# One-hot columns in quarters, dense products of the last tile ahead of its pairs, and two joins of picked rows at other places of a macro tile

## The reference

```
e = stack([tbl_0[ids[:, 0]], ..., tbl_25[ids[:, 25]]], axis=1)          # 2048 x 26 x 128
combined = concatenate([dense[:, None, :], e], axis=1)                  # 2048 x 27 x 128
inter = einsum('bfd,bgd->bfg', combined, combined)                      # 27 x 27 per sample
z = concatenate([dense, inter[:, iu, ju]], axis=1)                      # 351 pairs, f < g
h = concatenate([z, dense], axis=1)                                     # 607
h = maximum(h @ W_top1 + b_top1, 0.0)                                   # 512
h = maximum(h @ W_top2 + b_top2, 0.0)                                   # 256
y = h @ W_top3                                                          # 2048 x 1
```

## Time and profile before

| | |
|---|---|
| median of 3 runs | 451.1 us (450.58 to 453.02) |
| the profiled execution | 452.48 us, of which its span 450.7 us |
| PE busy | 413.7 us (92%) |
| DVE, ACT, POOL busy | 312.7, 255.1, 236.2 us (69%, 57%, 52%) |
| PE's granted clock, mean | 0.992 |

### The profile page before, as it was taken

How to read it: one execution, slowest core, us unless ns; L and a number is a source line. 1 busy time by engine, 2 the same in 40 slices (tenths; PEclk the granted TensorE clock), 3 DMA queues, 4 the chain that set the end, 5 groups by cost and what they waited for, 6 DMA issues and landing times.

```text
span 450.7 us, 9538 instructions
## 1 busy us (share of the span) xinstructions
PE 413.7 (92%) x3496; PEld 392.5 (87%) x3496; DVE 312.7 (69%) x970; ACT 255.1 (57%) x577; POOL 236.2 (52%) x247
## 2 busy tenths in 40 slices
PE   0867799989999999999999899999999999998997
PEld 1756699979998899989998799988999799988976
DVE  4898498786777857776777857777777876744351
ACT  3785667383455745375454844466452945459462
POOL 5677355555655566655566456555565556653000
PEclk9999699999999999999999999999999999999999
DMA  6999514232233172322522153221533243111000
GB/s 183 251 237 263 123 50 93 73 62 63 85 75 81 40 98 62 78 65 61 86 67 80 44 85 70 76 78 43 100 71 67 64 70 73 42 42 31 1 2 0
DMA packets 25407, 36.47 MB, mean 81 GB/s; under 512 B 6197, under 2 KB 19645, under 8 KB 25362
## 3 DMA queue, kind: packets, MB, share of 16 engines
q1 hardware_dynamic: 17682, 20.13, 21.7%
q0 software_dynamic: 7680, 15.74, 13.8%
HBM read 35.84 MB, written 0.01 MB: 80 GB/s over the span
## 4 chain that ended last, share of the span: by engine, by line
PE 75%; DVE 7%; issue 5%; DMA 4%; ACT 4%; SPq 3%; DVEq 0%; ACTq 0%
PE gram_ps L481 22%; PE x_ps L463 16%; PE x_ps L464 15%; PE tail_ps L521 5%; DVE hot L942 5%; PE tail_ps L522 5%; PE tail_ps L523 4%; PE x_ps L443 4%; DMA raws<-in_tbl_dram 4%; PE tail_ps L514 2%; SPq L349 2%; ACT x L695 2%; DVE pairs L926 1%; DVE gram L926 1%; ACT pairs L695 1%
## 5 line engine op out<-in xcount | busy, mean ns | idle before, releaser
L410 POOL DMA_INDIRECT rows<-in_tbl_dram,ids_sb x240 | 235.4, 981 | 178.7 <-PE x_ps L463 63.5
L942 DVE TENSOR_SCALAR hot<-ids_all,row_f 125x256 fp32r<-125x256 int32 x636 | 193.0, 373 | 51.8 <-PE x_ps L464 29.3
L463 PE MATMUL x_ps<-hot,table_hi 125*128 125x256 f32 x656 | 169.3, 294 | 23.4 <-DVE table_lo L929 10.2
L464 PE MATMUL x_ps<-hot,table_lo 125*128 125x256 f32 x656 | 164.0, 285 | 0.0
L463 PEld LDWEIGHTS x_ps<-hot,table_hi 125*128 125x128 f32 x656 | 126.2, 192 | 29.6 <-issue 20.0
L464 PEld LDWEIGHTS x_ps<-hot,table_lo 125*128 125x128 f32 x656 | 126.5, 193 | 0.0
L481 PE MATMUL gram_ps<-x 128*108 128x108 f32 x1024 | 108.3, 259 | 0.9 <-issue 0.9
L481 PEld LDWEIGHTS gram_ps<-x 128*108 128x108 f32 x1024 | 102.9, 175 | 2.0 <-ACT x L695 0.7
L695 ACT ACTIVATE picked<-x_ps 128x256 f32<-128x256 f32 x88 | 33.6, 382 | 97.7 <-PE x_ps L464 75.6
L695 ACT ACTIVATE gram<-gram_ps 44x208 f32<-44x208 f32 (+3 forms) x136 | 46.0, 338 | 29.1 <-PE gram_ps L481 24.3
L926 DVE COPY gram<-gram_ps 44x208 f32<-44x208 f32 (+1 forms) x120 | 44.3, 369 | 13.1 <-PE gram_ps L481 9.3
(11 more groups left out here) (82 smaller groups left out, 414.8 us busy)
## 6 DMA issues: line engine op xcount, KB each, us to landing
ids_all<-in_selected_ids_dram SPq DMA_DIRECT2D x83, 128.0 KB
raws<-in_tbl_dram SPq DMA_DIRECT2D x11, 448.0 KB
rows<-in_tbl_dram,ids_sb POOLq DMA_INDIRECT x240
rows<-in_r_dense_features_dram SPq DMA_DIRECT2D x16, 64.0 KB
stage<-in_W_pairs_dram SPq DMA_DIRECT2D x1, 702.0 KB
ids_start<-in_selected_ids_dram SPq DMA_DIRECT2D x5, 128.0 KB
raws<-in_tbl_dram SPq DMA_DIRECT2D x11, 52.0 KB
stage<-in_W_dense_dram SPq DMA_DIRECT2D x2, 256.0 KB
```

The lines of the kernel that those rows point to most:

```text
L410: pool.indirect_dma_start(out=rows[t][:, slot, :], out_offset=None, in_=tables[GATHERED[slot - 1]], in_offset=bass.IndirectOffsetOnAxis(ap ...
L463: first = pe.matmul(bank, table_hi[j][:, c, :], v, start=(c == 0), stop=False)
L464: last = pe.matmul(bank, table_lo[j][:, c, :], v, start=False, stop=(c == VC - 1))
L942: last = dve.tensor_scalar(hot_buffers[hot_place(number)][:, c, :], ids, row, None, ALU.is_equal)
```

## The change

- One-hot columns come in quarters of two chunks. `HOTS` is 4, at the start there are 10 places of half the size, so the memory is the same. PE waits at chunks 0, 2, 4 and 6 and tells after each of the first three quarters that it has been read. At the start ACT still makes the second half of every odd table, its last step now in two instructions of 512 columns instead of one of 1024.
- `picked` is split. Tables 0 to 5 have a second place for the rows of tile 1, used in turn by the macro tiles (`picked_a`), so pick 0 needn't follow `join(m, 1, 0)`. This join now stands behind pick 3.
- `join(m, 0, 1)` stands behind pick 0 of its macro tile instead of between the copies of rows (0,0) and (0,1); for macro tiles 0 and 7 it stays.
- In the last macro tile both joins of tile 1 are DVE's, ahead of its first pair columns; the dense products of layer 1 go to four banks of `gram_ps` and stand ahead of the pair transposes (n = 0, 1) and ahead of layer 3 of the macro tile before (n = 2, 3).

The diff, without the repeated renaming of halves to quarters:

```diff
-    HALF = VC // 2
-    HOTS = 2
+    HOTS = 4
+    QUARTER = VC // HOTS
-    START_HOTS = 5
-    ACT_HOTS = [2 * j + 1 for j in range(1, NS, 2)]
+    START_HOTS = 10
+    ACT_HOTS = [hot_number(0, j, h) for j in range(1, NS, 2) for h in range(HOTS // 2, HOTS)]
-    LAST_BANKS = [2, 3, 2, 3, 0, 2, 3, 1, 0, 2, 3, 1, 0, 2]
+    LAST_BANKS = [2, 3, 2, 3, 0, 2, 3, 4, 5, 6, 7, 1, 0, 2]
-        picked = sb("picked", [D, NS, MACRO])
+        picked_a = sb("picked_a", [D, 1 + 2, IDS, P])
+        picked_b = sb("picked_b", [D, NS - IDS, MACRO])
+        tail_banks += [b[:, i, :] for b in gram_ps for i in range(UNIT_BANKS)]
+        def picked_rows(m, t, part):
+            if part == 1:
+                return picked_b[:, :, t * P:(t + 1) * P]
+            return picked_a[:, 0 if t == 0 else 1 + m % 2, :, :]
-                    if c == HALF - 1:
+                    if c % QUARTER == QUARTER - 1 and c < VC - 1:
                         last.then_inc(hot_read, 1)
...
+            def layer1_dense(m, n):
+                if is_last(m):
+                    pe.wait_ge(gram_moved[n // UNIT_BANKS], (m + 1) * UNITS)
                 bank = tail_bank(m, Q_H1 + n)[:, 0:MACRO]
                 cols = slice(n * P, (n + 1) * P)
                 pe.wait_ge(dense_kept, m + 1)
                 add_product(bank, ...)
...
                 layer2(m - 1, 0)
+                layer1_dense(m, 0)
+                layer1_dense(m, 1)
                 pair_transposes(m, 0)
                 pair_transposes(m, 1)
                 layer2(m - 1, 1)
                 pair_transposes(m, 2)
                 pair_transposes(m, 3)
+                layer1_dense(m, 2)
+                layer1_dense(m, 3)
                 layer3(m - 1)
...
             def macro_tile(m, before):          # ACT
                 transposes(m, 0, 2)
-                join(m, 1, 0)
                 pick(m, 0)
+                if m > 0:
+                    join(m, 0, 1)
...
                 pick(m, 3)
+                join(m, 1, 0)
                 if not before:
                     split_w2()
...
                 transposes(m + 1, 0, 0)
-                join(m + 1, 0, 1)
+                if is_last(m + 1):
+                    join(m + 1, 0, 1)
                 transposes(m + 1, 0, 1)
...
             def last_tile(m):                   # ACT
-                join(m, 1, 0)
-                join(m, 1, 1)
...
+                for i in range(2):              # ACT, build_hot at the start
+                    number = hot_number(0, j, HOTS // 2 + i)
+                    wait_hot_read(act, hot_ahead(number))
+                    act.activation(hot_buffers[hot_place(number)], distance[:, i * QUARTER:(i + 1) * QUARTER, :],
+                                   ACT.Relu, bias=1.0, scale=-1.0).then_inc(act_hot_ready, 1)
...
             def last_tile(m):                   # DVE
                 gram_products(m - 1, TILES * UNITS - 1)
+                join(m, 0)
+                join(m, 1)
```

More of the change, by code:

```diff
@@ L213, in dlrm_kernel @@
         ids_all = sb("ids_all", [P, IDS, MACRO], I32)
-        hot = [sb(f"hot{i}", [VK, HALF, MACRO], F32R) for i in range(HOTS)]
+        hot = [sb(f"hot{i}", [VK, QUARTER, MACRO], F32R) for i in range(HOTS)]
         table_raw = [raws[:, j] for j in range(NS)]
-        HOT = HALF * MACRO
+        HOT = QUARTER * MACRO
         hot_buffers = [h[:] for h in hot]
@@ L274, in dlrm_kernel @@
         paced = sem("paced")
-        tail_moved = [sem(f"tail_moved{i}") for i in range(4)]
+        tail_moved = [sem(f"tail_moved{i}") for i in range(4 + N1)]
         stored = sem("stored")
@@ L351, in wait_hots @@
             def wait_hots(m, j):
-                for h in range(2):
+                for h in (HOTS // 2 - 1, HOTS - 1):
                     sp.wait_ge(*hot_done(hot_number(m, j, h)))
@@ L530, in layer1 @@
                             start=True).then_inc(paced, 1)
+            def layer1(m, n):
+                if not is_last(m):
+                    layer1_dense(m, n)
+                bank = tail_banks[tail_at(m, Q_H1 + n)[0]][:, 0:MACRO]
+                cols = slice(n * P, (n + 1) * P)
                 for c in range(KC):
@@ L708, in pick @@
             def pick(m, j):
-                if isinstance(m, int) and m < 0:
+                if j % IDS == 0:
+                    wait(act, joined[0], 2 * m + j // IDS + 1)
+                    wait(act, joined[1], 2 * m + 2 * (j // IDS))
+                into = m + 1
+                if m < 0:
                     m, k = 0, start_use(j)
                 else:
-                    if j % IDS == 0:
-                        act.wait_ge(joined[1], 2 * m + j // IDS + 1)
                     k = x_use(m, "table", j)
@@ L718, in pick @@
                 src = x_ps[bank][:].rearrange("p a b -> p (a b)")[:, 0:MACRO]
-                copy(picked[:, j, :], src).then_inc(x_moved[bank], 1)
+                if j < IDS:
+                    second = 1 + into % 2
+                    src = src.rearrange("p (t b) -> p t b", t=TILES)
+                    copy(picked_a[:, 0:second + 1:second, j, :], src).then_inc(x_moved[bank], 1)
+                else:
+                    copy(picked_b[:, j - IDS, :], src).then_inc(x_moved[bank], 1)
             def join(m, t, part):
-                j0, j1 = part * IDS, min((part + 1) * IDS, NS)
+                j1 = min((part + 1) * IDS, NS)
                 wait(act, gram_filled, (m - 1) * (TILES * UNITS) + (t + 1) * UNITS)
@@ L729, in join @@
                         act.wait_ge(x_moved[i], x_before(max(m - 1, 0), k + 1, i))
-                copy(x_slots(t, 1 + NG + j0, 1 + NG + j1).rearrange("d b f -> d f b"),
-                     picked[:, j0:j1, t * P:(t + 1) * P]).then_inc(joined[t], 1)
+                copy(joined_slots(t, part), picked_rows(m, t, part)).then_inc(joined[t], 1)
             def keep_dense(m):
@@ L886, in build_hot @@
             def build_hot(j):
[L888 removed]
+                built = j // 2
                 ids, loaded = ids_of(0, j)
                 act.wait_ge(*loaded)
[L892 to L895 removed]
+                wait(act, act_hot_ready, 2 * built)
+                for c in range(VC // 2):
+                    row = VC // 2 + c
+                    last = act.activation(distance[:, c, :], ids, ACT.Abs, bias=minus_row[0:VK, row:row + 1])
                 last.then_inc(distances_ready, 1)
[L897 to L900 removed]
+                act.wait_ge(distances_ready, built + 1)
+                for i in range(2):
[3 more added lines that the diff above has]
+                                   ACT.Relu, bias=1.0, scale=-1.0).then_inc(act_hot_ready, 1)
             act.wait_ge(iota_ready, 1)
@@ L934, in build_hot @@
                 dve.wait_ge(*loaded)
-                for h in range(2):
+                for h in range(HOTS):
                     number = hot_number(m, j, h)
@@ L939, in build_hot @@
                     wait_hot_read(dve, hot_ahead(number))
-                    for c in range(HALF):
-                        row = row_f[0:VK, h * HALF + c:h * HALF + c + 1]
+                    for c in range(QUARTER):
+                        row = row_f[0:VK, h * QUARTER + c:h * QUARTER + c + 1]
                         last = dve.tensor_scalar(hot_buffers[hot_place(number)][:, c, :], ids, row, None, ALU.is_equal)
@@ L1035, in split_w1d_low, with join @@
                 dve.wait_ge(ones_ready, 4)
+            def join(m, part):
+                j1 = min((part + 1) * IDS, NS)
+                dve.wait_ge(gram_filled, m * (TILES * UNITS))
+                for i in range(2):
+                    dve.wait_ge(x_moved[i], x_before(m - 1, x_use(m - 1, "table", j1 - 1) + 1, i))
+                copy(joined_slots(1, part), picked_rows(m, 1, part)).then_inc(joined[1], 1)
             def last_tile(m):
                 gram_products(m - 1, TILES * UNITS - 1)
+                join(m, 0)
+                join(m, 1)
                 pair_transposes(m - 1, 1)
```

37 lines of the change are left out of this document (15 added, 22 removed).

## The result

The changed kernel took 445.66 us (median of 4 executions, 445.26 to 446.99). The kernel before took 451.08 (4 executions, 450.58 to 453.02). The ratio is 0.988, with a 95% interval of 0.984 to 0.991: faster by 5.4 us, against 6.05 forecast.

A forecast was written before the change was run, and what follows sets the result against it. PE, busy 92% of the span, bounds the kernel, so time is won only where it idles. 3.15 + 1.25 + 0.5 + 0.35 + 1.1 - 0.3 = 6.05 us, to 445.1 us; own range 443.5 to 446.8, 8 in 10 441.5 to 449.0.

The forecast's parts named there:

- Five boundaries: Start of pick 10 to start of select 2, five times: 9.03 us in place of 9.66 on the mean, 3.15 us won.
- Select 2 at T + 9.03: T is the start of pick 10; ACT's chain through pick 0, join, pair columns and copy of rows ends there.
- the two joins change places and the end of ACT's chain stays where it was: At the five boundaries: ACT's copy of rows before select 2 ends near T + 9.03, before at T + 9.01.
- First boundary: Boundary without layer 3: without the join select 0 starts at 92.8 and select 2 at 99.3, not 100.55; 1.25 us won.
- Macro tile 0: Quarters win 0.6 and 0.6 at selects 2 and 9; the join of six behind pick 3 loses 0.7; net 0.5 us.
- The start: Last half of table 10: quarters leave four matmuls, 0.48 us, less 0.13 for ACT's split step; 0.35 won, 0 to 0.8 possible.
- The end: Layer 1 of the last macro tile: nine dense matmuls of 0.12 leave the chain, 1.1 us won, range 0.8 to 1.3.
- Waits and increments: In 88 selects, quarters add 176 waits and 176 increments, 2 ns each: 0.3 us lost.
- the rival that made the kernel slower: Waits and increments inside selects break the overlap of weight load and matmul, 17.6 us lost at 0.1 each: 462; chance 0.04.
- ACT's chain takes all back: Pick 0 and the join behind it come later than thought; all boundaries win nothing: 449.4 us; chance 0.12.
- ACT isn't the limit: Pair columns and pick 0 run tighter, and the 0.7 us before select 2 goes too: 440.9 us; chance 0.1.
- The clock rival: Half-clock stretch around 49 to 56 us, some 3 us: 442 without it, 448 if twice as long; chance 0.14.

The follow-up runs named there:

- the other traces with halves: Traces of the kernel before with only the last macro tile's dense products early (450.53 us), and with only 176 waits and increments added (451.42 us).
- the repeated run: The changed kernel again, not edited, beside its parts on the same chip: 444.26 us, ratio 0.984 to the kernel before.
- the end alone: Against the kernel before, only the last macro tile's dense products of layer 1 early; halves and old places of the joins: 450.53 us, ratio 0.999.

## Why the prediction was right, and where it was off

The time was right, 445.7 where 445.1 was forecast, in its own range of 443.5 to 446.8. It is right for the reason given in the large terms, each of which was forecast somewhat too large: like for like the change is worth 5.1 to 5.4 us and not 6.05. In macro tile 0 two misses cancel, which is luck, and the start isn't to be told.

**Five boundaries (3.15 forecast, 2.67 by the windows for which it was made).** That two orders ran beside each other, and that without DVE's part ACT's chain sets select 2, is shown: quarters alone and moved joins alone take the boundary to 9.16 and 9.45, both together not below 9.44. Select 2 at T + 9.03 was measured at T + 9.13. The sum of durations failed by 0.10 only, five times: 48.30 to 45.63. The spans give 3.38. Of this 0.36 is that pick 10 came later behind select 10 in two boundaries of before, and 0.36 lies outside the boundaries; beside the other traces with halves it is 2.7 to 2.9. "A wait for ACT's copy of rows stays in front of select 2" holds, but for 0.23 us, and at the weight load only. The other 0.72 stands one step earlier, at the pair transposes that wait for the eight pair columns, which I hadn't forecast. It is the same chain of ACT, one link before. The copy of rows ends 0.05 us before select 2 starts, as the chain said.

**What the step "the two joins change places and the end of ACT's chain stays where it was" missed.** True in sum, for two things cancel. The second place frees pick 0 from the end of the join, 0.26 us a boundary; the new places of the joins take 0.28 away, as the join of five now stands behind pick 0. With the joins unmoved the boundary would have been 9.16. With the join of five one line higher, ahead of pick 0, it is 8.5. I had the numbers for that: ACT's wait for select 0 stood in my chain as 2.2 us and I filled it with nothing. By the traces that one line is worth 5.3 us from the end of select 10 of macro tile 0 to that of macro tile 6 (305.72 to 300.39), as much as the whole change.

**First boundary (1.25, measured 1.00).** Select 0 starts 2.24 us behind select 10 and select 2 8.92, where 9.92 stood. The 1.13 of the spans has 0.13 from behind the boundary.

**Macro tile 0 (0.5, measured 2.21 between the two traces, 0.54 like for like).** Three things make the 2.21.

- The clock, 0.9. With one stretch at half clock there the changed kernel takes 43.05 us, with two (the repeated run) 43.93. Before had two, after one.
- A wait that only this trace of before has, 0.8. From the last matmul of select 8 to that of select 9 it takes 4.21 us, and 3.45 in the three other traces with halves, as with quarters. I priced the 0.53 of select 9 at 0.6 for the quarters. The row puts it down to "issue", and not to DVE as I read it. DVE's columns were late there, behind a wait of its own that the other three don't show; why it came is open:

```profile
82.27 1.58 DVE L926 COPY gram<-gram_ps 44x208 f32<-44x208 f32 x4 [0.95 <-PE gram_ps L481]
```

- The change itself, 0.54: 43.59 in the trace of the end alone (halves, one stretch) to 43.05. From the start of select 0 to the end of select 2 that is 0.8 (8.84 to 8.03), where 0.6 was forecast. Select 9 gives nothing, where 0.6 was forecast. The join of six takes back 0.25, where 0.7 was forecast: select 6 does wait for pick 5 as said (0.68 idle), but quarters win 0.39 in the same place (3.05 to 2.66), which I had written off.

So the term came out at its number because a gain that wasn't there and a loss that was set too high cancel.

**The start (0.35, measured -0.56).** Between 20 and 47 us ACT waits 3.5 us before and 4.4 us after for tables to arrive, so their arrival has a part in it; that it decides isn't shown. Over all traces, select 10 ended between 44.45 and 46.69 us, with no order by kernel. Half a microsecond is not to be found in that, and the two profiles say nothing on this term.

**The end (1.1, measured 1.01; 0.7 to 1.4 alone).** The quarter step of 1.07 us came as worked out.

**Waits and increments (-0.3).** Nothing, by the starts of the matmuls (118 and 119 ns with and without them), and the rival that made the kernel slower is out.

**The rivals.** "ACT's chain takes all back" had its mechanism right in kind, as ACT's chain is the limit, but took only what was forecast. "ACT isn't the limit" is out for the changed kernel, and is nearly what one moved line makes of it: 440.3 against its 440.9. The clock rival was real: 1.4 us a stretch, in any execution. The forecast took it for something that the change may shift. But PE's stalls stayed where they were (select 0 starts 4.69 us behind select 10 before and after), and still the stretch near 50 us is 3.4 or 6.8 us long for one program. Its price of some 3 us was near: 2.3 us for 6.8 us at half clock (9.73 and 7.45).

## What to carry to other kernels

Where two engines' orders between the same two events are nearly equal, cutting one wins only down to the other, so walk both to the end before pricing either; parts that shorten each by the same amount don't add. When a job is moved off a chain, look for the chain's own idle time: the same job ahead of the wait was free, and behind it cost about 0.9 us at each boundary. A wait in one trace may be that execution's own: a second trace of the same code would have shown that select 9 has none. Before trusting a gain under 1%, compare executions with equal mean clock, since here each stretch at half clock moved the time by more than the smaller edits did.

## What the runs showed of the hardware

- PE's clock fell to half near 50 us, around idle times of 1.1 to 2.2 us, and in the last macro tile behind idle times of 0.4 to 0.8 us, for 3.4 or 6.8 us, and only in some executions. Near 50 us, 23 transposes of no use in these idle times went with a full clock in all four traces that had them (without them in one of ten), and the median fell by 2.2 us. The Trainium skill ("TensorE: Matmul & The Clock Gate", section "Part 4: PE-mode transpose") says that transposes don't count as work of PE in the way that other matmuls do. Here the trace disagrees: filled with transposes of float32 tiles alone, the stalls were followed by a granted clock of 1.00.
- 176 waits that hold and 176 increments, on matmuls 0.12 us apart, cost no time that can be measured (ratio 1.0014, 0.9993 to 1.0036; the matmuls start as far apart as without them).
- An instruction of ACT that waits for the end of ACT's own copy starts 0.03 to 0.08 us after it, one that doesn't starts 0.24 us before it (247.26 and 247.50): some 0.3 us for a wait on one's own engine.
- The same two joins took 0.92 and 0.93 us on DVE and 1.75 and 1.48 (medians) on ACT:

```profile
394.60 0.92 DVE L966 COPY x<-picked_a 128x768 f32<-128x768 f32 x1
395.54 0.93 DVE L966 COPY x<-picked_b 128x640 f32<-128x640 f32 x1
```
